# Two transformer layers in one Trainium2 program: weights of the third projection fetched a stage earlier, turned rows in two copies, a list of rows built by 16-bit products

## What is computed

```python
x = x + _layernorm(_L0_attn_ref(_layernorm(x), W_qkv, b_qkv, W_out, b_out))       # a: 16 heads of 16, causal
x = x + _layernorm(_L0_ffn_ref(_layernorm(x), Wr, br, W1, W2, Ws1, Ws2))          # b: 32 experts, top 6 of 4 groups
x = x + _layernorm(_L1_attn_ref(_layernorm(x), W_attn, W_proj, lambdas...))       # c: difference of two score maps
x = x + _layernorm(_L1_ffn_ref(_layernorm(x), ln_w, ff_ln_w, wq, wk, wv, wo, gate_w, w1, w3, w2))
```

```python
h = rmsnorm(x, ln_w)
q = apply_rope((h @ wq).reshape(B, S, 16, 128)); k = apply_rope((h @ wk).reshape(B, S, 4, 128)); v = h @ wv
x = softmax(causal(q @ k.T / sqrt(128))) @ v @ wo + x
top_vals, top_idx = top_k(rmsnorm(x, ff_ln_w) @ gate_w, 2)
out = sum over e of gate_e * ((silu(h @ w1[e]) * (h @ w3[e])) @ w2[e])
```

## Time and profile before

| what | value |
|---|---|
| median of 3 executions | 2304.18 us |
| profiled execution | 2309.83 us |
| its span, first to last instruction | 2308.0 us |
| busy: PE, PEld, DVE, ACT, POOL | 85%, 64%, 68%, 47%, 33% |
| mean granted TensorE clock (1 is full) | 0.872 |
| narrow projections (stretches of PE and DVE work) | 11 to 70 us and 816 to 879 us |
| output stage of c | 1112.7 to 1147 us |
| grouped projection | 1147 to 1327 us |
| list of rows | 1850.7 to 1885 us |

### The profile page before, as it was taken

How to read it: one execution, slowest core, us unless ns; L and a number is a source line. 1 busy time by engine, 2 the same in 40 slices (tenths; PEclk the granted TensorE clock), 3 DMA queues, 4 the chain that set the end, 5 groups by cost and what they waited for, 6 DMA issues and landing times. The chain is left out here.

```text
span 2308.0 us, 38865 instructions
## 1 busy us (share of the span) xinstructions
PE 1967.3 (85%) x11554; PEld 1478.7 (64%) x11554; DVE 1563.1 (68%) x3874; ACT 1091.1 (47%) x2322; POOL 761.5 (33%) x809
## 2 busy tenths in 40 slices
PE   7699985899999776888588889999979849999990
PEld 4344445799999742333366656666659849999990
DVE  6555526788888876887478746666644468888874
ACT  2244443444444422777410056666643127777761
POOL 3122212655555430000145744545520012222211
PEclk9655555999999976999889989999989759999995
DMA  4422100000000033221145523232345145555533
GB/s 154 121 58 58 44 9 29 19 21 25 27 18 18 0 120 114 66 68 34 38 134 126 149 98 112 93 116 93 114 164 192 45 159 185 216 224 204 201 116 114
DMA packets 89936, 224.84 MB, mean 97 GB/s; under 512 B 14376, under 2 KB 28456, under 8 KB 84720
## 3 DMA queue, kind: packets, MB, share of 16 engines
q1 hardware_dynamic: 81584, 207.18, 27.0%
q0 software_dynamic: 4416, 12.06, 1.7%
q10 hardware_dynamic: 3840, 4.46, 0.7%
HBM read 157.59 MB, written 64.75 MB: 96 GB/s over the span
## 5 line engine op out<-in xcount | busy, mean ns | idle before, releaser
L559 POOL TENSOR_SCALAR d_att_probs<-d_att_probs,d_att_rinv 128x128 f32<-128x128 f32 (+2 forms) x192 | 177.0, 922 | 187.9 <-DVE d_att_rinv L583 187.9
L2357 DVE SCALAR_TENSOR_TENSOR b_acc<-bank,b_moe_gates,b_acc 128x256 f32<-128x256 f32 x512 | 212.4, 477 | 39.3 <-PE bank L2209 38.1
L2314 POOL TENSOR_TENSOR b_moe_act_low<-b_moe_act,b_moe_act_high 128x512 fp32r<-128x512 f32 x136 | 179.1, 1317 | 174.9 <-ACT b_moe_act_high L2266 174.9
L578 DVE CUSTOM_DVE_ANT_0 wide<-wide,d_att_later 128x128 f32<-128x128 f32 (+3 forms) x256 | 127.3, 497 | 136.2 <-PE wide L458 136.2
L514 ACT ACTIVATE d_att_probs<-wide,d_att_nmax 128x128 f32<-128x128 f32 (+3 forms) x256 | 133.2, 522 | 167.2 <-DVE d_att_nmax L578 167.2
L458 PE MATMUL wide<-d_att_k,d_att_q 128*128 128x128 f32 (+3 forms) x512 | 183.3, 441 | 13.3 <-DMA d_att_k<-k_dram 12.9
L1913 PE MATMUL wide<-e_moe_hT_high,e_moe_w_high 128*128 128x256 f32 x644 | 183.5, 285 | 3.5 <-DVE e_moe_hT_low L1992 3.5
L1913 PE MATMUL wide<-e_moe_hT_low,e_moe_w_high 128*128 128x256 f32 x644 | 183.3, 285 | 0.0
L1913 PE MATMUL wide<-e_moe_hT_high,e_moe_w_low 128*128 128x256 f32 x644 | 183.1, 284 | 0.0
L936 DVE TENSOR_REDUCE c_att_rmax<-wide 128x2 f32<-128x1024 f32 x128 | 155.1, 1223 | 38.9 <-PE wide L718 37.9
L932 DVE CUSTOM_DVE_ANT_0 wide<-wide,a_att_later 128x128 f32<-128x128 f32 (+3 forms) x256 | 120.9, 516 | 87.6 <-PE wide L718 82.8
(11 more groups left out here) (375 smaller groups left out, 5582.5 us busy)
## 6 DMA issues: line engine op xcount, KB each, us to landing
e_w<-in_e_w SPq DMA_DIRECT2D x23, 2688.0 KB, 9.9
q_dram<-d_in_rot SPq DMA_DIRECT2D x64, 256.0 KB, 3.4
d_att_q<-q_dram SPq DMA_DIRECT2D x16, 1024.0 KB, 4.9
o_dram<-d_att_o SPq DMA_DIRECT2D x64, 256.0 KB, 2.0
d_out_oT<-o_dram SPq DMA_DIRECT2D x16, 1024.0 KB, 5.7
b_moe_w<-in_b_w SPq DMA_DIRECT2D x17, 512.0 KB, 3.5
a_q<-q_parts SPq DMA_DIRECT2D x96, 64.0 KB, 2.1
c_q<-q_parts SPq DMA_DIRECT2D x96, 64.0 KB, 2.1
```

Source lines behind the costliest of these rows:

```text
L559: g.tensor_scalar(tile, tile, rinv[:, j, qt:qt + 1], None, ALU.mult).then_inc(scaled, 1)
L2314: g.tensor_tensor(ap[1][:, u % 4, :], act[:, u % 4, :], ap[0][:, u % 4, :], ALU.subtract).then_inc(act_low, 1)
L2357: nv.scalar_tensor_tensor(out=tile, in0=y, scalar=gate, in1=tile, op0=ALU.mult, op1=ALU.add).then_inc(acc_done, 1)
```

## The change

The narrow projections keep the turned rows in two buffers, used in turn; ScalarE no longer waits for the values of the sequence before. TensorE turns the next sequence after the third of four value tiles instead of after the fourth, and all four groups are written out.

```diff
-        hT = sb("hT", [P, KT, S])
+        hT = [sb(f"hT{i}", [P, KT, S]) for i in range(2)]
...
                         a.wait_ge(tr_done, b * KT + k + 3)
-                        if k == 0:
-                            a.wait_ge(v_done, b * 2 + 2)
-                        nc.scalar.copy(hT[:, k, :], tr[k][:, :]).then_inc(hT_ready, 1)
+                        nc.scalar.copy(hT[b % 2][:, k, :], tr[k][:, :]).then_inc(hT_ready, 1)
...
                         if q % 2:
                             mm.then_inc(v_done, 1)
-                    if not last:
-                        turn(b + 1)
+                        if q == 2 and not last:
+                            turn(b + 1)
...
-                with pe.Fori(0, B - 1) as b:
-                    group(b, False)
-                group(B - 1, True)
+                for b in range(B):
+                    group(b, b == B - 1)
```

```diff
+    def load(self, sp):
+        sp.dma_start(self.raw_v, weights(self.w_v)).then_inc(self.w_in, 16)
+        sp.dma_start(self.col[:, :], self.col_in).then_inc(self.w_in, 16)
+        for i in range(2):
+            sp.dma_start(self.raw_qk[:, :, self.halves[i]], weights(self.w_qk)[:, :, self.halves[i]]).then_inc(self.qk_in[i], 16)
...
                 sp.dma_start(w[:, :, :], weights(w_out)).then_inc(w_in, 16)
                 if bias is not None:
                     sp.dma_start(bias_row[:, :], bias.partition_broadcast(P)).then_inc(w_in, 16)
+                ahead.load(sp)
...
-                for dst, src in ((raw_v, weights(a["d_wv"])), (col[:, :], a["d_ln"])):
-                    sp.dma_start(dst, src).then_inc(w_in, 16)
-                for i in range(2):
-                    sp.dma_start(raw_qk[:, :, halves[i]], weights(a["d_wqk"])[:, :, halves[i]]).then_inc(qk_in[i], 16)
                 sp.dma_start(rope[:, :, :, :], a["d_rope"]).then_inc(rope_in, 16)
...
-        oT = [sb(f"oT{i}", [P, 4, S]) for i in range(4)]
+        oT = [room[:, 4 * i:4 * i + 4, :] for i in range(4)]
```

```diff
-        at_lane = sb("at_lane", [P, PAIRS, P])
+        at_lane, of_tile = sb("at_lane", [P, PAIRS, P], BF16), sb("of_tile", [P, PAIRS, 2, TILES], BF16)
...
+            @block.scalar
+            def _(a):
+                a.wait_ge(table_in, 16)
+                a.wait_ge(tile_ready, 1)
+                nc.scalar.activation(of_tile[:, :, 1, :], at_tile[:, :, :], ACT.Copy, scale=this_lane).then_inc(parts_ready, 1)
...
+                pe.wait_ge(parts_ready, 2)
                 for i in range(PAIRS):
                     if i % CHUNK == 0:
                         pe.wait_ge(lane_ready, i // CHUNK + 1)
-                    mm = nc.tensor.matmul(where[:, 0:TILES], at_lane[:, i, :], at_tile[:, i, :], start=(i == 0), stop=(i == PAIRS - 1))
+                    mm = nc.tensor.matmul(where[:, 0:2 * TILES], at_lane[:, i, :], of_tile[:, i, :, :].rearrange("p j n -> p (j n)"),
+                                          start=(i == 0), stop=(i == PAIRS - 1))
...
-                link(nv.tensor_tensor(at_tile[:, :, :], at_tile[:, :, :], number.unsqueeze(2).to_broadcast([P, PAIRS, TILES]), ALU.mult))
+                nv.tensor_tensor(of_tile[:, :, 0, :], at_tile[:, :, :], number.unsqueeze(2).to_broadcast([P, PAIRS, TILES]),
+                                 ALU.mult).then_inc(parts_ready, 1)
...
-                link(nv.tensor_copy(held[:, :], where[:, 0:TILES]))
+                link(nv.tensor_copy(of_pair[:, :, :].rearrange("p j n -> p (j n)"), where[:, 0:2 * TILES]))
+                link(nv.scalar_tensor_tensor(out=held[:, :], in0=of_pair[:, 0, :], scalar=float(P), in1=of_pair[:, 1, :], op0=ALU.mult, op1=ALU.add))
```

More of the change, by code:

```diff
@@ L1004, with __init__ @@
 class ProjectionAhead:
-    def __init__(self, c, ctx, name, z):
+    def __init__(self, c, ctx, name, z, w_qk, w_v, col):
         self.c, self.z = c, z
+        self.w_qk, self.w_v, self.col_in = w_qk, w_v, col
+        self.rot = ctx.enter_context(c.nc.sbuf_tensor(f"{name}_rot", [P, H + KVH, S], F32))
+        self.raw_qk = self.rot[:, 0:10, :].rearrange("p c s -> p (c s)").rearrange("p (k n) -> p k n", k=KT)
+        self.raw_v = self.rot[:, 10:12, :]
+        self.col = ctx.enter_context(c.nc.sbuf_tensor(f"{name}_col", [P, KT], F32))
+        half = (H + KVH) * P // 2
+        self.halves = [slice(i * half, (i + 1) * half) for i in range(2)]
+        self.w_in, self.qk_in = c.sem(f"{name}_w_in"), [c.sem(f"{name}_qk_in{i}") for i in range(2)]
         self.norm_x, self.norm_z = Norm(c, ctx, name + "_x"), Norm(c, ctx, name + "_z")
@@ L2474, in build @@
         with ExitStack() as begun:
-            d_ahead = ProjectionAhead(c, begun, "d_in", z)
+            d_ahead = ProjectionAhead(c, begun, "d_in", z, a["d_wqk"], a["d_wv"], a["d_ln"])
             with ExitStack() as stage:
@@ L2495, in build @@
                 grouped_attention(c, "d_att", q_dram, k_dram, stored, vals, o_dram)
-                grouped_output(c, "d_out", o_dram, a["d_wo"], z)
+                grouped_output(c, "d_out", o_dram, a["d_wo"], z, d_ahead.rot)
         c.end_stage()
```

44 lines of the change are left out of this document (23 added, 21 removed).

## The result

The changed kernel took **2271.32 us** (median of 4 executions, 2265.12 to 2289.61) against 2305.05 for the kernel before beside it (4 executions, 2302.74 to 2306.73): ratio 0.9882, 95% interval 0.9851 to 0.9913. The forecast was 2283.5, range 2277.5 to 2291. The profiled execution took 2265.12 us, span 2263.3, against 2309.83 and 2308.0.

A forecast was written before the change was run, and what follows sets the result against it. No engine was taken to bound the whole program, so each edit was priced in its stage: -11.2 + 0.2 - 9.1 - 0.6 = -20.7 us, taking the median from 2304.18 to 2283.5 us, range 2277.5 to 2291.

The forecast's parts named there:

- List of rows, -9.1: List of rows: 16-bit products, paced by DVE's pieces, save 9.1 us net, ends 6.8 and 10.0.
- Rival (3): List of rows: 16-bit products cost a full old record, -6.8 instead of -9.1, total 2285.8 us; chance 0.09.
- Grouped projection, -11.2: Start of the grouped projection: weights fetched during the output stage save 11.2 us.
- rival (4): Grouped projection: clock stays low in the value tiles, -8.3 instead of -11.2, total 2286.4 us; chance 0.05.
- Output stage of c, +0.2: Output stage of c: SyncE's four further DMA issues cost 0.2 us, ends 0 and 0.9.
- rival (5): Output stage of c: its `c_out` weights land 3 us later beside the early weights, total 2286.3 us; chance 0.05.
- Narrow projections, -0.6: Both narrow projections: the earlier turn saves about 0.3 us each, 0.6 together, ends -5.2 and +2.
- The visible signs: Narrow projections: no gap behind the turn but one inside or before it, and DVE's rests later in the first group.
- Rival (1): Narrow projections: TensorE alone bounds them, -5.2 in place of -0.6, total 2278.9 us; chance 0.12.
- Rival (2): Narrow projections: stores bound them harder, +2 us, total 2286.1 us; chance 0.09.
- rival (7): Attention of c: stays at the low clock, +88 us, total about 2371 us; chance 0.03.
- rival (7)'s reverse: Attention of a: TensorE falls below DVE's 57.5 in 100, some -35 us in each 100; chance 0.01.

The follow-up runs named there:

- e1_narrow: The kernel before with only the narrow projections' edit (two buffers, earlier turn): 2302.73 us, ratio 1.0006.
- e3_list: The kernel before with only the 16-bit products for the list of rows: 2293.21 us, ratio 0.9976.
- e8_fill: The changed kernel with POOL's zero filling of `qs` and `ks` moved into the first two groups of the narrow projections: 2284.08 us, a single execution.
- e6_wide256: The changed kernel with the score rows of a's attention computed over at least 256 columns: 2283.50 us, ratio 0.9919.
- e2_preload: The kernel before with only the grouped projection's weights fetched early, in the output stage of c: 2293.66 us, ratio 0.9974.
- e5_two: The kernel before with early weights and 16-bit list, narrow projections left as before: 2280.28 us, ratio 0.9885.
- e10_two512: The kernel before with early weights, 16-bit list and a's attention score rows over all 512 keys, narrow projections as before: 2259.86 us, ratio 0.9836.
- the two comparisons: The first is the result above; the second is the changed kernel once more, nothing edited, 12 executions: 2289.48 us, ratio 0.9952.
- e7_wide512: The changed kernel with the score rows of a's attention computed over all 512 columns: 2254.06 us, ratio 0.9806.
- e9_before512: The kernel before with only the score rows of a's attention widened to all 512 keys: 2267.88 us, ratio 0.9872.

## Why the prediction was right, and where it was wrong

**List of rows, -9.1.** Right: -9.5 in the table, -9.7 to DVE's copy, less 0.24 for the added instruction. ScalarE's rounding took 1.52 us for the estimated 1.4, beside DVE's 1.69. A mis-sized step that cost nothing: I took 0.11 us a product from the weights' columns and 0.3 for the end, about 1.2 for eight, and the last eight took 0.80; only these count, since DVE's pieces pace the rest (TensorE waited 0.27 to 0.34 us for each after the first). Eight weight loads of this form span 0.59 us in the trace, some 0.07 each, at a granted clock of 0.50. Rival (3), a full old record each, is out.

**Grouped projection, -11.2.** The step fails in what it was subtracted from. Its forward reckoning held: query products 10.94 us after the first turn, measured 11.67; the 24 value products with 12 at the slow spacing of 0.43 us for the assumed 9 account for most of the rest (3 x 0.2 = 0.6), a part of what rival (4) had. But the -11.2 was taken against the earlier trace rows, one execution in which the weights landed late; the same code lands them 3.1 to 3.5 us sooner in three other profiles (7.6 to 8.0 for 11.1), and the stage's start is 5 to 6 us shorter there. The gain is about 7. Two hints were in hand: the profiled execution lay 5.65 us over the median, and the rows that held it back ended with a DMA. I subtracted from its span everything that it had lost to that landing, and then moved the difference over to a median that had not lost it.

**Output stage of c, +0.2.** Right as to the transfer: 2.9 us for 2.8, and rival (5) is out. But the stage's first result tile comes 3.1 us later, for another reason, which I hadn't listed: TensorE began it at a granted clock of 0.67 (1087.7 to 1098 us) and had 1.00 after that (to 1112 us), where the kernel before has 1.00 from the start (1112.7 to 1120 us) and needs 3.62 us for the same first sixteen products (timeline of the changed kernel):

```profile
1092.44 5.70 PE L1119 MATMUL bank<-c_out_w,c_out_oT 128*128 128x256 f32 x16
...
1098.85 3.62 PE L1119 MATMUL bank<-c_out_w,c_out_oT 128*128 128x256 f32 x16
```

Some of it comes back ahead (c's attention and projection 1.0 and 1.2 us shorter). `e1_narrow` has these 17.1 us too, `e3_list`, without the narrow edit, has 16.4, and `e8_fill` and `e6_wide256`, with it, have the usual 14.1. `e2_preload`, `e5_two` and `e10_two512`, with early weights, have 14.2, so it is no matter of these. Of the kept profiles six of the eight with the narrow edit begin this stage at the low clock and one of the six without. That is likely a part of what the edit costs; what decides it in one execution wasn't found.

**Narrow projections, -0.6.** The visible signs came out: a gap inside the turn in place of the one behind it, `h` stretched while POOL fills, the rests later, the third group of the first projection 0.65 sooner and the fourth 0.08. But what binds was put in the wrong place. I had `h` done at 41.7 and the rounding at 42.6, so that the stores would hold the groups; measured, `h` ends at 42.03 (2.80 us, where I had at hand the 2.14 of the kernel before) and the rounding at 42.24, and the copy still waits for the turn behind `h`. The groups became 12.95 and 12.76 us long where I had 12.76 and 12.22. The store loop binds only in `e8_fill`, once `h` is short again. The first projection is within 0.7 us of before; c's is 1.2 shorter, for the 0.3 that I gave it. TensorE was also busy 11.46 of its 12.27 us, not 11.2. Rival (1), TensorE alone, is out. Rival (2), +2, comes nearest to the whole effect of the edit, 2.1 to 2.6 us by the three pairs above, but not for its reason alone: a group is 0.3 to 0.7 us longer and not 1, and the rest lies behind the projections.

**Sum.** With what was measured: about -7 (projection), -9.5 (list), +2 (narrow edit, with c's stretches) is -14.5; the executions at equal clock give -13.6 and the common line -10.6, which is too little. The prediction had -20.7, of the 6.2 between them 4.2 are the late landing and 2.6 the narrow edit. The number of the first comparison, -33.7, was reached by 18 us of a clock that I gave no weight. The forecast lies between the two comparisons, but that confirms nothing: one was moved past it by chance of the clock, and the other stayed within the range although a third of the forecast gain wasn't there.

**The clock.** I wrote that the prediction is wrong "if the clock of either attention changes". It did, by rival (7)'s reverse, which had 0.01 and a price of -35 in each 100 us. Measured in the changed kernel's profile: 24.1 us less in that attention. About 68 us of its 233.6 stood at the high level, before 14 of 257.7, from which I estimate some -31 in each 100 us: the price was about right, the chance was not. Both chances, 0.03 for (7) and 0.01 for its reverse, were my estimates, held small because "three executions agreed within 0.2%". Three executions can't show a branch taken in one of five. Nor was rival (7)'s reverse a matter of this change: the kernel before takes it as well, in 15 of 73 executions (a mean clock of 0.880 or more). At the low level a's attention leaves TensorE few waits: it is busy 93 in 100 us in the stretch of the earlier trace rows, at 0.53, and never idle there for more than 1.1 us at a time. For telling the two branches apart busy time is the wrong measure, since the low clock itself raises it: in the same stretch of the changed kernel, at 0.84, it is 83. What brought the high one in the runs was the widening of the score products (0.885 or more in 22 of 22 executions, without it in 7 of 73 of the kernel before), by their width or by the work it adds; which of them, and how, wasn't shown.

## What to carry to other kernels

Before subtracting a wait that ended with a DMA, ask whether it is the usual one (here it belonged to a landing of 11.1 us, where three other profiles had 7.6 to 8.0): look at a second execution, or at the gap between the profiled time and the median. Where a long stage stands at the low clock with an engine 94% busy, as a's attention does here, treat its clock as a branch (15 of 73 executions of the kernel before had a mean of 0.880 or more, the highest, 0.894, with 2273.1 us for the median of 2302.8), give it a chance and a price, and never read a difference of medians of four executions without the mean clock beside it. And try widening that stage's products: one line, with more work for TensorE, was worth more here than the three edits together (35.6 us between medians for 13.6).

## What the hardware showed that I had not expected

- More work made the kernel faster. Score rows over 512 columns in place of 128 to 512 brought 35.6 us between medians in the kernel before (2303.47 to 2267.88), although at an equal clock they cost some 6 us (2307.2 for 2301.0, an estimate by the common slope).
- a's attention stood at the low clock (0.52 from 106 to 190 us of the kernel before) while TensorE was busy 78.94 of 84 us, and in the changed kernel it left it with its work the same (0.50 in those 84 us, 0.98 from 224 to 290 us). Read in rows of 4 us each, the profiles show single rows near the high level that fall back at once (0.93 at 212 us of the changed kernel, 0.50 in the next); the longest stretch at it is 28 us in `e2_preload`, 32 in `e3_list`, 64 in the changed kernel and 80 in `e7_wide512`. What begins such a run without the widening wasn't found.
- The same 1280 KB, issued behind the same 512 KB at the same place in the program, took 7.6, 7.7, 8.0 and 11.1 us at the median in four executions (`e3_list`, `e9_before512`, `e1_narrow`, kernel before). The 1536 KB of rotary factors took 12.0 to 16.3 us behind them in these four and 6.3 to 6.8 alone in the ten profiles with early weights.
- DVE's four instructions of `h` took 1.37 us alone (`e8_fill`) and 2.80 beside POOL's filling (changed kernel).
